# One core, sixteen graph batches two at a time: another table for the order in which two batches' stages are interleaved

## The reference, cut to what matters

```python
x = _layernorm(x + _L0_gnn_ref(x, adj, ...))   # one attention layer, ELU
x = _layernorm(x + _L1_gnn_ref(x, adj, ...))   # three layers: attention, norm, FFN 256->1024->256 (gelu), norm
x = _layernorm(x + _L2_gnn_ref(x, adj, ...))   # attention that keeps the 16 largest weights of a row, ELU
x = _layernorm(x + _L3_gnn_ref(x, adj, ...))   # eight heads of 32 columns, masked softmax, relu, projection
```

```python
e = leaky_relu(s1[:, None] + s2[None, :])      # 512 x 512
a = softmax(where(mask, e, -inf))              # L2: weights under the 16th largest of the row become 0
h = a @ v
```

## Time and profile before

| what | value |
|---|---|
| time, median of 3 runs | 4817.73 us (4815.55 to 4819.25) |
| the profiled execution | span 4814.6 us from its first to its last instruction; the run times are 1.0 to 4.7 us above it |
| instructions | 51354 |
| TensorE matmul busy | 3797.7 us (79%) |
| VectorE / ScalarE / GpSimd busy | 49% / 37% / 13% |
| mean granted TensorE clock | 0.882 of full speed |

### The profile page before, as it was taken

How to read it: one execution, slowest core, us unless ns; L and a number is a source line. 1 busy time by engine, 2 the same in 40 slices (tenths; PEclk the granted TensorE clock), 3 DMA queues, 4 the chain that set the end, 5 groups by cost and what they waited for, 6 DMA issues and landing times.

```text
span 4814.6 us, 51354 instructions
## 1 busy us (share of the span) xinstructions
PE 3797.7 (79%) x15680; PEld 2615.2 (54%) x15680; DVE 2380.4 (49%) x6205; ACT 1798.4 (37%) x3631; POOL 606.3 (13%) x364
## 2 busy tenths in 40 slices
PE   2778878787787878878787887878878787887866
PEld 1555555555555555555555555555555555555543
DVE  2255454545545455454545545455364545545543
ACT  1233334343443434334343443434334343433423
POOL 0111101111110101101111110101111111110100
PEclk8888988899898989988898898988989898898977
DMA  4001000010010101000010010101000010110101
GB/s 104 0 1 31 18 16 25 10 40 9 22 27 1 40 9 31 19 16 24 9 40 10 22 27 3 37 10 31 18 18 23 10 40 9 25 24 6 30 5 40
DMA packets 91198, 106.27 MB, mean 22 GB/s; under 512 B 25889, under 2 KB 57249, under 8 KB 90913
## 3 DMA queue, kind: packets, MB, share of 16 engines
q1 hardware_dynamic: 82464, 94.34, 7.7%
q0 software_dynamic: 8448, 8.39, 1.4%
HBM read 35.55 MB, written 8.39 MB: 9 GB/s over the span
## 4 chain that ended last, share of the span: by engine, by line
PE 49%; issue 24%; DVE 18%; POOL 4%; ACT 3%; SPq 1%; DVEq 0%; DMA 0%; POOLq 0%; ACTq 0%
PE acc L1070 9%; PE acc L1035 8%; PE work L1055 7%; PE work L1022 6%; PE acc L1114 6%; DVE stats L662 3%; PE work L989 3%; DVE T L591 3%; PE work L965 2%; PE work L946 2%; PE work L1084 2%; PE work L1098 2%; POOL R L484 1%; POOL rstd L476 1%; POOL R L481 1%
## 5 line engine op out<-in xcount | busy, mean ns | idle before, releaser
L1055 PE MATMUL work<-XT,w_sb 128*128 128x512 f32 x1536 | 718.3, 615 | 34.6 <-ACT XT L890 30.5
L1070 PE MATMUL acc<-w_sb,gT 128*128 128x256 f32 x3072 | 695.5, 380 | 6.1 <-ACT gT L899 6.1
L476 POOL TENSOR_TENSOR rstd<-var_eps,minus_half 128x4 f32<-128x4 f32 x160 | 171.9, 1074 | 3993.1 <-DVE var_eps L670 3993.1
L1070 PEld LDWEIGHTS acc<-w_sb,gT 128*128 128x128 f32 x3072 | 578.7, 190 | 131.6 <-issue 43.8
L655 DVE COPY PT<-work 128x512 f32<-128x512 f32 x416 | 286.4, 689 | 517.7 <-PE work L1022 516.1
L868 ACT ACTIVATE PT<-work 128x512 f32<-128x512 f32 x416 | 247.4, 595 | 736.0 <-PE work L1022 734.1
L1055 PEld LDWEIGHTS work<-XT,w_sb 128*128 128x128 f32 x1536 | 299.3, 198 | 360.8 <-issue 345.2
L899 ACT ACTIVATE gT<-work,b_sb 128x512 f32<-128x512 f32 x384 | 261.9, 686 | 580.1 <-PE work L1055 580.0
L1035 PE MATMUL acc<-X,PT 128*128 128x256 f32 x1536 | 402.6, 426 | 95.8 <-ACT PT L868 95.8
L1022 PE MATMUL work<-ident,T 128*128 128x128 f32 x2304 | 366.6, 310 | 138.1 <-DVE row_max L764 50.8
L1022 PEld LDWEIGHTS work<-ident,T 128*128 128x128 f32 x2304 | 295.7, 159 | 230.8 <-issue 69.6
(11 more groups left out here) (123 smaller groups left out, 4948.9 us busy)
## 6 DMA issues: line engine op xcount, KB each, us to landing
q<-R SPq DMA_DIRECT2D x256, 64.0 KB, 2.0
k<-X SPq DMA_DIRECT2D x256, 64.0 KB, 2.0
k<-neg SPq DMA_DIRECT2D x256, 64.0 KB, 2.0
q<-HX SPq DMA_DIRECT2D x256, 64.0 KB, 2.0
HX<-in_x SPq DMA_DIRECT2D x16, 512.0 KB, 3.6
neg<-in_adj POOLq DMA_DIRECT2D x16, 512.0 KB, 6.7
out<-X SPq DMA_DIRECT2D x16, 512.0 KB, 6.0
w_sb<-in_L_gnn_W SPq DMA_DIRECT2D x6, 1024.0 KB, 8.9
```

What stands on the lines that cost most here:

```text
L1055: last = pe.matmul(u.bank[:], w1_sb[:, l, c, f * P:(f + 1) * P], XT[s][:, c, :], start=(c == 0), stop=(c == DC - 1))
L1070: last = pe.matmul(acc[s][t // 2][:, t % 2, :], gT[:, f % (FC // 2), t * P:(t + 1) * P], w2_sb[:, l, f, :], start=(f == 0 and t % 2 == 0), ...
```

## The change

The table HALF is another one. Every stage of it is in both tables, once; the engines' functions, the tiles, the semaphores and the loops are the same. In the queues, TensorE's order differs at some thirty stages, VectorE's at a dozen, ScalarE's at half a dozen; those of GpSimd and SyncE are the same. The core of the diff:

```diff
-        ("middle", "L0", "v2"), ("ending", "L1.2", "ffn1c ffn2b"), ("middle", "L0", "bc alphaz lrelu"),
-        ("ending", "L1.2", "ffn1d"), ("middle", "L0", "exp"), ("ending", "L1.2", "ffn2c ffn2d"),
...
-        ("ending", "L2", "xT"), ("middle", "L1.0", "xT s bc"), ("ending", "L2", "v1"),
-        ("middle", "L1.0", "alphaz lrelu"), ("ending", "L2", "v2"), ("middle", "L1.0", "exp"),
-        ("ending", "L2", "bc"), ("middle", "L1.0", "pT1"), ("ending", "L2", "topk alphaz"),
-        ("middle", "L1.0", "pT2 agg"), ("ending", "L2", "lrelu exp pT1 pT2 agg"),
-        ("middle", "L1.0", "sum norm hT ffn1a"), ("ending", "L2", "sum norm"), ("middle", "L1.0", "ffn1b"),
-        ("ending", "L3", "xT v1 v2 q k"), ("middle", "L1.0", "ffn2a"), ("ending", "head0", "stack"),
-        ("middle", "L1.0", "ffn1c ffn2b"), ("ending", "head0", "scores1"), ("middle", "L1.0", "ffn1d"),
...
-        ("middle", "L1.1", "s"), ("ending", "head2", "scores2"), ("middle", "L1.1", "bc"),
-        ("ending", "head1", "pT1 pT2 pv"), ("middle", "L1.1", "alphaz lrelu"), ("ending", "head2", "exp"),
...
-        ("ending", "head2", "pT2"), ("middle", "L1.1", "agg"), ("ending", "head3", "exp"),
-        ("middle", "L1.1", "sum"), ("ending", "head4", "scores1 scores2"), ("middle", "L1.1", "norm"),
-        ("ending", "head3", "pT1 pT2"), ("middle", "L1.1", "hT"), ("ending", "head4", "exp"),
...
-        ("middle", "L1.2", "hT"), ("ending", "L3", "ysum norm load store"), ("starting", "L0", "masks xT"),
-        ("middle", "L1.2", "ffn1a ffn1b ffn2a"), ("starting", "L0", "v1"),
+        ("middle", "L0", "v2"), ("ending", "L1.2", "ffn1c"), ("middle", "L0", "bc alphaz"),
+        ("ending", "L1.2", "ffn2b ffn1d ffn2c ffn2d"), ("middle", "L0", "lrelu exp pT1"),
...
+        ("middle", "L0", "norm"), ("ending", "L2", "xT"), ("middle", "L1.0", "xT"), ("ending", "L2", "v1"),
+        ("middle", "L1.0", "s bc alphaz lrelu"), ("ending", "L2", "v2 bc topk"), ("middle", "L1.0", "exp pT1"),
+        ("ending", "L2", "alphaz lrelu"), ("middle", "L1.0", "pT2 agg"), ("ending", "L2", "exp pT1"),
+        ("middle", "L1.0", "sum"), ("ending", "L2", "pT2"), ("middle", "L1.0", "norm"), ("ending", "L2", "agg"),
+        ("middle", "L1.0", "hT ffn1a"), ("ending", "L2", "sum"), ("middle", "L1.0", "ffn1b"),
+        ("ending", "L2", "norm"), ("ending", "L3", "xT v1"), ("middle", "L1.0", "ffn2a ffn1c"),
+        ("ending", "L3", "v2 q k"), ("ending", "head0", "stack"), ("middle", "L1.0", "ffn2b ffn1d"),
+        ("ending", "head0", "scores1"), ("middle", "L1.0", "ffn2c"), ("ending", "head1", "stack"),
+        ("ending", "head0", "scores2"), ("ending", "head2", "stack"), ("middle", "L1.0", "ffn2d"),
+        ("ending", "head0", "exp"), ("middle", "L1.0", "xsum"), ("ending", "head1", "scores1 scores2"),
+        ("middle", "L1.0", "xnorm"), ("ending", "head0", "pT1"), ("ending", "head3", "stack"),
...
+        ("ending", "head1", "pT1"), ("middle", "L1.1", "bc"), ("ending", "head1", "pT2"),
...
+        ("ending", "head5", "stack"), ("ending", "head2", "pT2"), ("ending", "head3", "exp"),
+        ("ending", "head4", "scores1 scores2"), ("ending", "head3", "pT1 pT2"),
+        ("middle", "L1.1", "agg sum norm"), ("ending", "head4", "exp"), ("ending", "head3", "pv"),
+        ("ending", "head6", "stack"), ("ending", "head5", "scores1"), ("middle", "L1.1", "hT ffn1a"),
+        ("ending", "head5", "scores2"), ("middle", "L1.1", "ffn1b ffn2a"), ("ending", "head4", "pT1 pT2"),
+        ("ending", "head5", "exp"), ("middle", "L1.1", "ffn1c"), ("ending", "head7", "stack"),
+        ("ending", "head6", "scores1"), ("middle", "L1.1", "ffn2b"), ("ending", "head6", "scores2"),
+        ("middle", "L1.1", "ffn1d"), ("ending", "head5", "pT1"), ("middle", "L1.1", "ffn2c"),
+        ("ending", "head5", "pT2"), ("middle", "L1.1", "ffn2d xsum"), ("ending", "head5", "pv"),
...
+        ("ending", "head7", "pT1"), ("middle", "L1.2", "bc"), ("ending", "head7", "pT2"),
...
+        ("ending", "L3", "norm"), ("middle", "L1.2", "ffn1b ffn2a"), ("ending", "L3", "load store"),
+        ("starting", "L0", "masks xT v1"),
```

More of the change, by code:

```diff
@@ L89, in build @@
     HALF = [
[3 rows of a table removed]
-        ("ending", "L1", "l1sum"), ("middle", "L0", "agg sum"), ("ending", "L1", "norm"), ("middle", "L0", "norm"),
-        ("ending", "L2", "xT"), ("middle", "L1.0", "xT s bc"), ("ending", "L2", "v1"),
-        ("middle", "L1.0", "alphaz lrelu"), ("ending", "L2", "v2"), ("middle", "L1.0", "exp"),
-        ("ending", "L2", "bc"), ("middle", "L1.0", "pT1"), ("ending", "L2", "topk alphaz"),
-        ("middle", "L1.0", "pT2 agg"), ("ending", "L2", "lrelu exp pT1 pT2 agg"),
-        ("middle", "L1.0", "sum norm hT ffn1a"), ("ending", "L2", "sum norm"), ("middle", "L1.0", "ffn1b"),
[3 rows of a table removed]
@@ L102, in build @@
-        ("ending", "head2", "stack"), ("ending", "head0", "exp"), ("ending", "head1", "scores1"),
-        ("middle", "L1.0", "ffn2d xsum"), ("ending", "head1", "scores2"), ("ending", "head0", "pT1"),
-        ("ending", "head3", "stack"), ("middle", "L1.0", "xnorm"), ("ending", "head1", "exp"),
[5 rows of a table removed]
-        ("ending", "head2", "pT2"), ("middle", "L1.1", "agg"), ("ending", "head3", "exp"),
[5 rows of a table removed]
-        ("ending", "head5", "exp"), ("middle", "L1.1", "ffn2b"), ("ending", "head7", "stack"),
-        ("ending", "head6", "scores1"), ("middle", "L1.1", "ffn1d ffn2c"), ("ending", "head6", "scores2"),
@@ L118, in build @@
-        ("ending", "head5", "pT1 pT2"), ("middle", "L1.1", "ffn2d"), ("ending", "head5", "pv"),
-        ("middle", "L1.1", "xsum"), ("ending", "head7", "scores1"), ("middle", "L1.1", "xnorm"),
[3 rows of a table removed]
-        ("middle", "L1.2", "alphaz lrelu exp"), ("ending", "head7", "pv"), ("middle", "L1.2", "pT1"),
-        ("ending", "L3", "heads"), ("middle", "L1.2", "pT2 agg sum norm"), ("ending", "L3", "proj"),
-        ("middle", "L1.2", "hT"), ("ending", "L3", "ysum norm load store"), ("starting", "L0", "masks xT"),
@@ L126, in build @@
-        ("middle", "L1.2", "ffn1a ffn1b ffn2a"), ("starting", "L0", "v1"),
+        ("middle", "L0", "v2"), ("ending", "L1.2", "ffn1c"), ("middle", "L0", "bc alphaz"),
+        ("ending", "L1.2", "ffn2b ffn1d ffn2c ffn2d"), ("middle", "L0", "lrelu exp pT1"),
+        ("ending", "L1.2", "xsum"), ("middle", "L0", "pT2"), ("ending", "L1.2", "xnorm"),
+        ("middle", "L0", "agg"), ("ending", "L1", "l1sum"), ("middle", "L0", "sum"), ("ending", "L1", "norm"),
+        ("middle", "L0", "norm"), ("ending", "L2", "xT"), ("middle", "L1.0", "xT"), ("ending", "L2", "v1"),
@@ new lines, in build @@
+        ("middle", "L1.0", "s bc alphaz lrelu"), ("ending", "L2", "v2 bc topk"), ("middle", "L1.0", "exp pT1"),
+        ("ending", "L2", "alphaz lrelu"), ("middle", "L1.0", "pT2 agg"), ("ending", "L2", "exp pT1"),
+        ("middle", "L1.0", "sum"), ("ending", "L2", "pT2"), ("middle", "L1.0", "norm"), ("ending", "L2", "agg"),
[6 rows of a table added]
+        ("middle", "L1.0", "xnorm"), ("ending", "head0", "pT1"), ("ending", "head3", "stack"),
[3 rows of a table added]
+        ("middle", "L1.1", "alphaz"), ("ending", "head1", "pv"), ("middle", "L1.1", "lrelu exp"),
@@ new lines, in build @@
+        ("ending", "head2", "exp"), ("ending", "head4", "stack"), ("ending", "head3", "scores1 scores2"),
+        ("middle", "L1.1", "pT1"), ("ending", "head2", "pT1"), ("middle", "L1.1", "pT2"),
+        ("ending", "head5", "stack"), ("ending", "head2", "pT2"), ("ending", "head3", "exp"),
+        ("ending", "head4", "scores1 scores2"), ("ending", "head3", "pT1 pT2"),
+        ("middle", "L1.1", "agg sum norm"), ("ending", "head4", "exp"), ("ending", "head3", "pv"),
+        ("ending", "head6", "stack"), ("ending", "head5", "scores1"), ("middle", "L1.1", "hT ffn1a"),
@@ new lines, in build @@
+        ("ending", "head5", "scores2"), ("middle", "L1.1", "ffn1b ffn2a"), ("ending", "head4", "pT1 pT2"),
+        ("ending", "head5", "exp"), ("middle", "L1.1", "ffn1c"), ("ending", "head7", "stack"),
[3 rows of a table added]
+        ("ending", "head7", "scores1"), ("ending", "head6", "exp"), ("middle", "L1.1", "xnorm"),
[3 rows of a table added]
+        ("middle", "L1.2", "alphaz"), ("ending", "head7", "pv"), ("middle", "L1.2", "lrelu exp pT1"),
+        ("ending", "L3", "heads"), ("middle", "L1.2", "pT2 agg"), ("ending", "L3", "proj"),
+        ("middle", "L1.2", "sum norm hT"), ("ending", "L3", "ysum"), ("middle", "L1.2", "ffn1a"),
```

## The result

The new table gives 4788.23 us (median of 4 runs, 4780.34 to 4795.93) against 4818.25 before (4 runs): a ratio of 0.994, 95% interval 0.9926 to 0.9954. It is 30 us faster, where I had forecast 27 us slower. The profiled execution has a span of 4794.3 us, 20 us under the one before; it is the slowest of the four (4795.93), so the trace shows 20 us of the 30. The lines of kernel.py are two higher than before.

What follows compares the result with a forecast made beforehand. TensorE's own queue, its work, waits and half-clock time, was taken as the bound. Terms summed to +1.8 us a half, times 15 = +27 us: 4845 us, 0.6% slower, range 4785 to 4900.

Steps and rivals of the forecast that it cites:

- rival A: Both aggs run at 2.4 GHz, so the clock losses go: -2.6 us a half, 4779 us; chance 0.28, half way included.
- top-k, with v1: L1.0's agg all behind the top-k, L2's v1 ahead of L1.0's s and bc: +2.4 us a half.
- heads 0 and 1: ffn2a and ffn1c ahead of v2, a DMA wait, xsum's tail ahead of head 1's maxima: +1.4 us a half.
- bc behind pT1, both: Copies of pT1 no longer behind bc's maxima: -1.4 us a half at head 1, -0.2 at head 7.
- L1.1's agg: Agg moved behind head 3's pT, slower with the clock priced in: +1.3 us a half, bounds -0.4 and +4.
- L1.1's FFN: FFN stretch with heads 4 and 5 falls from 34.3 to 33.1 us: -1.2 a half.
- L0's xT: Moved behind ffn2a into the wait for the masks, v1 and v2 less at half clock: -0.5 us a half.
- of 0 to 3.4 I take 1.5: Delay in us of L1.0's bc and alphaz from v1 at half clock ahead of them, up to 3.4.
- agg's loss: Clock loss of L1.0's agg after idling behind the top-k: 2.7 us, ending it at 954.3.
- The part without the clock: L1.1's agg to ffn1a takes 21.4 us against 21.8 before: -0.4 a half.
- my working left it 0.3: Heads 0 and 1 without the 1.15 us DMA wait: +0.3 us a half, xsum's tail ahead of head 1's maxima.
- its limit of 2.6: Rival A decides once clock losses of the two aggs and ffn1a together fall under 2.6 of 4.4 us.

Runs made afterwards that it cites:

- the two single exchanges: L2's v1 ahead of L1.0's s and bc in the kernel before: 4811.64 us; old L1.0 and L2 order, v1 still early, in heads_as_before: 4728.46 us.
- heads_as_before: The new table with the stretch from L3's xT to head 0's pT1 in the order of before: 4723.09 us.
- ffn_moved_back: The new table with ffn2a and ffn1c behind head 0's stack again, xsum still ahead of head 1's maxima: 4734.62 us.
- ffn_as_before: heads_as_before with L1.1's FFN and the heads 4 to 6 beside it in the order of before: 4754.7 us.
- heads_new_in_before: The table of before with only the new stretch of heads 0 and 1: 4846.36 us.

## Why the prediction was wrong

Its sign was wrong: 4788 lies 3 us inside the lower end of the range, on the side of rival A. The terms in us a half, as forecast, as the two traces show the stretch, and as undoing the part gives it (the run's difference by 15):

| term | forecast | in the traces | by undoing |
|---|---|---|---|
| top-k, with v1 | +2.4 | -1.4 | -0.7 |
| heads 0 and 1 | +1.4 | +3.0 | +4.3 |
| bc behind pT1, both | -1.6 | -0.9 at head 1 | -0.2 |
| L1.1's agg | +1.3 | +0.7 | -1.2 |
| L1.1's FFN | -1.2 | -1.0 | -2.1 |
| L0's xT | -0.5 | -0.8 | -1.3 |

By its own steps:

- *Top-k, "of 0 to 3.4 I take 1.5".* This is the step that failed first, and the term that is off the most. I priced v1 at half clock ahead of s and bc, so that bc and alphaz come later. L2's bc came 1.5 us earlier after the wait: with v1 directly behind the wait the stretch has a granted clock of 0.85 in place of 0.61, s takes 1.84 and not 3.58, and alphaz no longer stands behind v1's copy, which I had named and given no price. Exchanged alone in the kernel before it gains 6 us. With agg's loss at 1.9 instead of 2.7, and a mean of 7.6 for the FFN blocks instead of 8.8, the term of +2.4 is -1.4 (L2's xT to L3's xT), or -11 us by the two single exchanges, of which the second (5 us) can't be told from zero.
- *L1.1's agg, +1.3.* The part without the clock, -0.4, had the right sign, and undoing it shows -1.2. I added 1.7 for a clock that pieces of idle time would lower. They didn't: agg took 7.27 and ffn1a 3.70.
- *Heads 0 and 1, +1.4.* The mechanism was right in part (1.07 of DMA wait, 3.32 ahead of head 1's maxima), its size was not: 3.0 a half in the trace, 4.3 by undoing. I had only the stretch itself in the sum; of the 4.1 between the traces of after and heads_as_before 1.3 lie behind it, and of the 4.4 to ffn_moved_back's 2.1. In the new table the xsum tail costs nothing, where my working left it 0.3, as a wait of 3.28 stood ahead of the transposes before.
- *FFN, -1.2.* Right in the trace (-1.0), 2.1 by undoing. The 1.28 us change of table left no wait ahead of ffn1d. The Trainium skill's 2.66 us ("ScalarE: Activation LUTs", What ACT_TABLE_LOAD costs) would have left one of 1.6 by my working.
- *bc behind pT1, -1.6 together.* The wait ahead of pv fell from 4.4 to 3.02 as forecast, and the gain by undoing is 3 us in all. The shorter wait was not time: pv behind it takes 6.59, where it took 5.79.
- *L0's xT, -0.5.* 20 us by undoing, 1.3 a half, within the bounds I gave. In the traces v1 and v2 of L0 take a mean of 4.4 us and not 6.05.

Two slips in the working change nothing: 954.3 is 2.3 behind 952.0 and not 2.4, and 4718.32 less 4710.3 is 8.02.

Rival A had the sign and named the clock. The losses that it lets go, 4.4 us, measured 2.2 (1.9 in L1.0's agg, 0.2 and 0.1 in L1.1's agg and ffn1a), under its limit of 2.6. But L1.0's agg did not run at full clock, and by my own sum the 2.2 give only -0.4 a half, -6 us. That rival A's 4779 lies near the result is in part luck: its terms are off both ways, in the traces the top-k by -1.1 and heads 0 and 1 by +1.6. The Trainium skill ("TensorE: Matmul & The Clock Gate", What's actually happening), cited for rival A, puts the ramp's penalty for modelling under 1% of a typical span. That does not hold here: two fillings of waits with useless work gave 29 and 28 us, 1.2% of the 4723.

The parts undone in heads_as_before or alone (6 + 5 + 18 + 32 + 3 + 20) make 84 of its 94 us; the rest is L0's stretch, which was not tried alone, and what doesn't add. Why parts don't add is argued, not shown: the slow clock falls on other work whenever something ahead shifts, as in head 1's pv.

## What to carry to other kernels

Where a queue has waits of 8 to 10 us, try large matmuls straight behind the wait and small work after them, and useless matmuls in the wait itself: filling two such waits gave 29 and 28 us here, the exchange alone 6. Count the clock as part of a wait's price, but read it from the trace, stage by stage: L1.1's agg behind pieces of idle time under 1 us lost 0.2 us, head 1's pv behind 3.02 us of waiting lost 3.0. Keep independent blocks as cover between the members of a chain in which each waits for the last, as DMA, scores and maxima do, and not ahead of the chain. And don't trust a sum of stretches within 1%: undo each part on the chip. In this kernel one part cost 32 us in one table and 65 in another, and only by undoing it was it found that the new table carried a loss twice its net gain.

## What the runs showed of the hardware beyond that

Halves of a round last 276.5, 279.9, 283.4, 286.8 or 290.1 us in most of the profiled executions, steps of some 3.4 us with hardly a value between. In ffn_as_before (280.9 to 285.2) and heads_new_in_before they do not. No run shows where the steps come from. Added work of 41 us cost 20. The kernel before varies by 3 to 7 us between the runs of a group, the kernel after by 16.
